# Passage from layer 2 to layer 3 of a four-layer graph network: attention vectors, half of the first attention sums, and the loads and casts of two weights moved to earlier places

## The reference, cut to what matters

```python
def _L2_gnn_ref(x, adj_matrix, bond_matrix, Wq, bq, Wk, bk, Wv, bv, Wo, bo, seq_len):
    q, k, v = (proj(Wq, bq), proj(Wk, bk), proj(Wv, bv))      # 8 heads of 64
    scores = jnp.einsum('bhqd,bhkd->bhqk', q, k) * SCALE
    mask = (adj_matrix + bond_matrix)[:, None, :, :]
    attn = jax.nn.softmax(scores * mask, axis=-1)
    ctx = jnp.einsum('bhqk,bhkd->bhqd', attn, v)
    return jnp.einsum('bse,fe->bsf', ctx.transpose(0, 2, 1, 3).reshape(...), Wo) + bo

def _L3_gnn_ref(X, A, Wv, bv, aw, ab, Wk, bk):
    Xw = X @ Wv + bv
    sj, si = Xw @ aw[:d, 0], Xw @ aw[d:, 0]
    e = jax.nn.leaky_relu(sj[:, None, :] + si[:, :, None] + ab[0], negative_slope=0.2)
    alpha_matrix = A * jnp.exp(e)
    transition = alpha_matrix / (jnp.sum(alpha_matrix, axis=-1, keepdims=True) + 1e-12)
    H, Xk = 0, X
    for k in range(3):
        H = H + Xk @ Wk[k] + bk[k]
        Xk = jnp.einsum('bij,bjd->bid', transition, Xk)
    return jax.nn.relu(H)
```

## Time and profile before

| what | value |
|---|---|
| runs, median of 3 | 2360.78 us |
| lowest and highest run | 2358.31 and 2362.7 us |
| the profiled execution | 2360.88 us |
| its span in the trace | 2359.1 us |
| mean granted TensorE clock | 0.996 |
| TensorE busy | 2323.2 us (98%) |
| VectorE busy | 1352.4 us (57%) |
| ScalarE busy | 798.0 us (34%) |
| POOL busy | 807.1 us (34%) |
| DMA, mean over the span | 89 GB/s |

### The profile page before, as it was taken

The page is one execution under the profiler, slowest core; times in us unless marked ns, Lnnn a source line. Parts: engine busy times, 40 slices in busy tenths (PEclk is TensorE's granted clock), DMA queues, the critical chain, the costliest instruction groups (busy, mean ns, idle before and its releaser), DMA issues. The chain is left out here.

```text
span 2359.1 us, 39284 instructions
## 1 busy us (share of the span) xinstructions
PE 2323.2 (98%) x15823; PEld 1898.6 (80%) x15823; DVE 1352.4 (57%) x2602; ACT 798.0 (34%) x1429; POOL 807.1 (34%) x995
## 2 busy tenths in 40 slices
PE   8999999999999999999999999999989999999998
PEld 5688888888888878888888888888768888888887
DVE  3565566566655654444555444555677667676753
ACT  3333333334333343333333333333332222223221
POOL 2454454445544524222333222333352222212120
PEclk9999999999999999999999999999999999999999
DMA  6323333333333333222223222222444333434330
GB/s 194 78 65 92 94 112 90 91 89 81 84 93 100 106 112 113 76 59 59 61 72 90 72 60 59 60 74 84 131 106 113 82 107 86 103 85 106 82 90 36
DMA packets 173477, 208.97 MB, mean 89 GB/s; under 512 B 64800, under 2 KB 81264, under 8 KB 173296
## 3 DMA queue, kind: packets, MB, share of 16 engines
q1 hardware_dynamic: 173296, 206.48, 31.7%
HBM read 88.91 MB, written 50.37 MB: 59 GB/s over the span
## 5 line engine op out<-in xcount | busy, mean ns | idle before, releaser
L328 PE MATMUL bank<-w_hi,h3T_hi 128*128 128x512 f32 x768 | 302.4, 394 | 0.0
L328 PE MATMUL bank<-w_lo,h3T_hi 128*128 128x512 f32 x768 | 299.5, 390 | 0.0
L328 PE MATMUL bank<-w_hi,h3T_lo 128*128 128x512 f32 x768 | 299.4, 390 | 0.0
L613 DVE TENSOR_TENSOR Z_lo<-bank,Z_hi 128x512 fp32r<-128x512 f32 x128 | 87.2, 682 | 192.4 <-ACT Z_hi L956 192.4
L328 PEld LDWEIGHTS bank<-w_lo,h3T_hi 128*128 128x128 f32 x768 | 144.4, 188 | 30.3
L328 PEld LDWEIGHTS bank<-w_hi,h3T_hi 128*128 128x128 f32 x768 | 144.5, 188 | 30.2
L328 PEld LDWEIGHTS bank<-w_hi,h3T_lo 128*128 128x128 f32 x768 | 144.4, 188 | 30.2
L956 ACT ACTIVATE Z_hi<-bank 128x512 fp32r<-128x512 f32 x128 | 76.0, 596 | 252.9 <-PE bank L328 163.3
L613 DVE TENSOR_TENSOR cT_lo<-bank,cT_hi 128x256 fp32r<-128x256 f32 x128 | 44.7, 408 | 203.7 <-ACT cT_hi L956 203.7
L646 DVE STREAM_TRANSPOSE hs<-hn 128x512 f32<-128x512 f32 x192 | 123.5, 687 | 58.1 <-ACT hn L970 58.1
L1203 POOL TENSOR_TENSOR h3T_lo<-hGA,h3T_hi 128x512 fp32r<-128x512 f32 x64 | 82.6, 1326 | 206.1 <-ACT h3T_hi L956 206.1
(11 more groups left out here) (231 smaller groups left out, 6053.5 us busy)
## 6 DMA issues: line engine op xcount, KB each, us to landing
hGA<-hs SPq DMA_DIRECT2D x768, 64.0 KB, 2.0
mid<-x SPq DMA_DIRECT2D x32, 1024.0 KB, 4.8
x<-mid SPq DMA_DIRECT2D x32, 1024.0 KB, 5.8
x<-in_x SPq DMA_DIRECT2D x16, 1024.0 KB, 5.9
hGB<-hs SPq DMA_DIRECT2D x256, 64.0 KB, 2.0
out<-x SPq DMA_DIRECT2D x16, 1024.0 KB, 5.4
blk<-in_adj SPq DMA_DIRECT2D x128, 64.0 KB, 2.9
adj<-in_adj SPq DMA_DIRECT2D x64, 64.0 KB, 4.1
```

The lines of the kernel that those rows point to most:

```text
L328: ins = eng.matmul(b[:], h[l][:, k, ts], W[r][:, k, :], start=(k == 0 and i == 0), stop=(last and k == 3 and i == 2))
L613: return eng.tensor_tensor(lo, src, hi.bitcast(F), ALU.subtract)
```

## The change

Nothing is computed otherwise; operations change their places in the programs of VectorE, ScalarE, POOL and SP. TensorE's program is as before.

- VectorE, iteration 15: the attention vectors and `cst` stand first, ahead of `l2_ctx(14, 0)` and the statistics. `l3_sums(0, (0, 1))` stands behind `l2_ctx(14, 1)`, ahead of output (14,1) and the softmax, and writes its unused product to sc3; `l3_sums(0, (2, 3))` stands ahead of V's evictions. Before, all of them stood between V's evictions.
- VectorE, iteration 16: `adj_T(3, 0)` and `l3_alpha(0)` stand behind the transposes of (3,1), ahead of outputs (15,2) and (15,3). Of group 1's sums two tiles stand behind the outputs, the third behind the row sum of group 0, the fourth behind T_lo of group 0.
- VectorE, layer 3, group 0: `adj_T(3, 1)` and `l3_alpha(1)` stand ahead of the transposes of (3,2) and the last `l3_zlo`.
- ScalarE: the hi parts of W3[2] and W3[1] are cast between the two halves of the last softmax's exponents; before, W3[2] behind the ptc copies, W3[1] behind the second norm. `l3_exp(0)` stands right behind that norm. The hi features of (3,0) wait for the first four sums.
- POOL: the lo part of W3[1] is made ahead of `l3_alpha(0)`.
- SP: W3[2] and W3[1] are asked ahead of the gather of (3,0). `rows3` is cut in two: `sums_out3(0)` and the adjacency blocks stand in iteration 15 behind the store of x, ahead of the load of W3[0]; `sums_in3(0)` stands in iteration 16.

```diff
             for g in range(NG + 1):
                 on, prev = g < NG, g >= 1
-                if prev:
-                    l2_ctx(g - 1, 0)
-                else:
-                    l01_recip(NG - 1)
-                    l01_x2(NG - 1, range(4))
-                stats_A(*(after2(g) if on else (3, 1)))
                 if g == NG - 1:
                     dve.wait_ge(d_vec3, 64)
...
                     eng.tensor_tensor(cst, cst, abc, ALU.add).then_inc(v_cst, 1)
                 if prev:
+                    l2_ctx(g - 1, 0)
+                else:
+                    l01_recip(NG - 1)
+                    l01_x2(NG - 1, range(4))
+                stats_A(*(after2(g) if on else (3, 1)))
+                if prev:
                     l2_out(g - 1, 0)
                 if on:
                     transposes(*after2(g))
                 if prev:
                     l2_ctx(g - 1, 1)
+                if g == NG - 1:
+                    l3_sums(dve, eng, 0, (0, 1))
...
                     elif u == 0:
                         transposes(3, 1)
+                        adj_T(3, 0)
+                        l3_alpha(0)
                 if not on:
-                    adj_T(3, 0)
-                    l3_alpha(0)
-                    l3_sums(dve, eng, 1, range(4))
+                    l3_sums(dve, eng, 1, (0, 1))
                 if on:
                     dve.wait_ge(d_bv2, 16)
+                    if g == NG - 1:
+                        l3_sums(dve, eng, 0, (2, 3))
...
-                        if g == NG - 1 and t >= 1:
-                            l3_sums(dve, eng, 0, ((0,), (1,), (2, 3))[t - 1])
...
                     if g == 0 and t == 0:
                         l3_rowsum(0)
+                        l3_sums(dve, eng, 1, (2,))
                     if g == 0 and t == 1:
                         l3_tlo(0)
+                        l3_sums(dve, eng, 1, (3,))
...
                     if t == 3 and g + 2 < NG:
+                        if g == 0:
+                            adj_T(3, 1)
+                            l3_alpha(1)
                         transposes(3, g + 2)
                     l3_zlo(1, ("z1", g, t), g, t)
-                if g + 1 < NG:
+                if g and g + 1 < NG:
                     adj_T(3, g + 1)
-                l3_alpha(g + 1)
+                    l3_alpha(g + 1)
...
+            first = g == 0 and 0 in ts
             if g == 0:
-                dve.wait_ge(*bank.done(("qk", NG - 1, 3)))
+                dve.wait_ge(v_cst, 1)
+                if not first:
+                    dve.wait_ge(*bank.done(("qk", NG - 1, 3)))
...
-                    dve.wait_ge(v_dotA, 8 * g + 2 * t + c - 1)
-                    eng.scalar_tensor_tensor(yt[c][:] if g < 2 else junk[:, c, :], hn[t][:], 0.0, arow[:, c, :], ALU.max, ALU.mult,
+                    dve.wait_ge(v_dotA, 8 * g + 2 * t + c - (not first))
+                    unused = sc3[:] if first else yt[c][:] if g < 2 else junk[:, c, :]
+                    eng.scalar_tensor_tensor(unused, hn[t][:], 0.0, arow[:, c, :], ALU.max, ALU.mult,
...
                 if not on:
                     norm_A(3, 1)
+                    l3_exp(0)
...
                 if on:
                     l2_exp(g, 0)
-                if on:
+                    if g == NG - 1:
+                        split_in_place(W3[2], d_w2)
+                        split_in_place(W3[1], d_w1)
                     l2_exp(g, 1)
-                else:
-                    split_in_place(W3[1], d_w1)
-                    l3_exp(0)
...
-                    act.wait_ge(v_cst, 1)
+                    act.wait_ge(v_dotA, 4)
                     features2_hi(3, 0, hT3[0])
...
-                if g == NG - 1:
-                    split_in_place(W3[2], d_w2)
...
+            split_in_place(W3[1], "w1")
             l3_alpha(0)
-            split_in_place(W3[1], "w1")
             l3_rowsum(0)
...
-            def rows3(g):
+            def sums_out3(g):
                 if g < NG:
                     sp.wait_ge(v_sc, g + 1)
                     eng.dma_start(si_dr[g].rearrange("(t p) -> p t", p=128), scol[g % 2][:, :, 1], allow_slow_non_contiguous=True).then_inc(d_sc, 16)
+
+            def sums_in3(g):
+                if g < NG:
                     sp.wait_ge(d_sc, 16 * (g + 1))
...
+                if g == NG - 1:
+                    sp.wait_ge(*bank.done(("k2", g, 3)))
+                    eng.dma_start(W3[2]["raw"][:], rows(L3_gnn_Wk[2])).then_inc(d_w2, 16)
+                    eng.dma_start(W3[1]["raw"][:], rows(L3_gnn_Wk[1])).then_inc(d_w1, 16)
                 if g == 0:
                     sp.wait_ge(v_x2, 4 * NG)
                     store_x(kA(0, NG - 1), mid[0][NG - 1])
                 if on:
                     gather(*after2(g))
-                if g == NG - 1:
-                    sp.wait_ge(*bank.done(("k2", g, 3)))
-                    eng.dma_start(W3[2]["raw"][:], rows(L3_gnn_Wk[2])).then_inc(d_w2, 16)
-                    eng.dma_start(W3[1]["raw"][:], rows(L3_gnn_Wk[1])).then_inc(d_w1, 16)
                 if g == NG:
-                    load_blocks(3, 0)
-                    rows3(0)
+                    sums_in3(0)
                     gather(3, 1)
                 if prev:
                     sp.wait_ge(v_x3, 4 * g)
                     store_x(kA(2, g - 1), mid[1][g - 1])
                 if g == NG - 1:
+                    sums_out3(0)
+                    load_blocks(3, 0)
                     sp.wait_ge(*bank.done(("pT", g, 3)))
                     eng.dma_start(W3[0]["raw"][:], rows(L3_gnn_Wk[0])).then_inc(d_w0, 16)
...
-                rows3(g + 1)
+                sums_out3(g + 1)
+                sums_in3(g + 1)
```

## The result

| | before | after |
|---|---|---|
| median of 14 runs | 2360.81 us | 2357.26 us |
| lowest and highest | 2358.31, 2362.7 us | 2351.14, 2359.18 us |
| the profiled execution | 2360.88 us | 2352.77 us |

The ratio is 0.9980, with a 95% interval of 0.9973 to 0.9986: 3.5 us faster, where 11.8 had been forecast. The spread tells more than the median. The 14 runs after fall into two groups with nothing between them: four at 2351.1 to 2352.8 us, ten at 2356.5 to 2359.2. The profile shows an execution of the shorter group, so it alone does not explain the median.

What follows compares the result with a forecast made beforehand. TensorE, busy 2323 of 2359.1 us, bounds the kernel, so only its idle and slow time can be won: 6.1 + 0.7 + 5.0 + 0.4 = 12.2 us off 2360.88 gives 2348.7, stated as 2349.0, range 2345.5 to 2355.0.

Steps and rivals of the forecast that it cites:

- Code still comes late: Rival: code for context (15,1) still late, o2(15,0) starts as before, later gains mostly hold; 2353.4 us, chance 0.12.
- Stall (a): TensorE's 4.41 us stop inside context (15,1), laid to cT_lo or late code; output o2(15,0) starts sooner, gaining 6.1 us.
- It moves the waits only: Rival: each wait feeds the next, so less than 4.7 us are won; 2358 us, chance 0.05.
- si's round trip: Store and read-back of si ahead of group 1's row sum in layer 3; rows landed by 1751.5 to 1753 us.
- row sum 1: Row sum of layer 3's group 1, waiting for alpha(1); the wait stays near 2.3 us, 0.4 us won.
- Attention vectors, W1, W2 and the gather: Vectors moved into VectorE's idle time, W2 and W1 asked 20 us sooner, gather of (3,0) sooner; vectors cost nothing.
- First sums: Sums (0,1) ahead of VectorE's last softmax, (2,3) ahead of V's evictions; cost taken as 0, at most 3.3 us.
- Row sum 0: Row sum of layer 3's group 0, waiting for alpha(0); wait falls from 1.43 to about 0.7 us, gaining 0.7 us.
- The hop: TensorE's first hop in layer 3, waiting for T_lo; its wait and half clock behind it go, gaining 5.0 us.
- the first rival: Row sum of layer 3's group 1 waits over 3 us and the clock falls; 2351.3 us, chance 0.2.
- Collision of sums and POOL: Rival: VectorE's sums slow beside POOL, 1.08 us more each, T_lo late, hop waits 4.6 us; 2355.5 us, chance 0.06.
- arow late: Rival: VectorE blocks on arow at the head of its softmax, delaying context (15,0); 2365.6 us or more, chance 0.02.

Runs made afterwards that it cites:

- e1: The changed kernel once more with no edit: 2358.32 us, 11 runs, three at 2350.2 to 2352.3 and eight at 2358.3 to 2360.4.
- e2: The changed kernel with the load of W3[0] asked about 8 us later, ahead of the gather of (3,1): 2358.25 us, nine of 11 runs long.
- e6: The changed kernel with group 0's adjacency block loads issued only behind context (15,1), the si store left early: 2361.42 us, 11 of 12 runs long.
- e10: The changed kernel with W2 and W1 asked and cast where they were before, plus 32 identity transposes at TensorE's start: 2348.42 us, ratio 0.9944.
- e3: The changed kernel with W2 and W1 asked and cast where they were before: 2352.6 us in 10 runs, ratio 0.9967.
- e11: The kernel before the change with 32 identity transposes added at TensorE's start: 2361.11 us, 11 runs, ratio 0.9999.
- e9: The changed kernel with 32 identity transposes at TensorE's start and POOL's two bias sums moved behind the scales of (3,2): 2348.84 us.
- e12: The changed kernel with 32 identity transposes at TensorE's start and the second half of the first sums behind V's evictions: 2352.57 us.
- e5: The changed kernel with group 0's si store issued only behind context (15,1), which also let the adjacency loads go out sooner: 2352.3 us, five runs.
- e7: The changed kernel with both group 0's si store and its adjacency block loads issued only behind context (15,1): 2354.86 us, six runs.
- e16: The changed kernel with 8 identity transposes (16 instructions) added at TensorE's start: 2351.4 us, five runs from 2350.5 to 2351.6.
- e17: The changed kernel with two 1 MB memory-to-memory copies added ahead of the si store: 2353.4 us, five runs from 2352.4 to 2354.1.
- e4: The kernel before the change with its first four transposes done nine times, shifting later code by 64 instructions: 2366.18 us.

## Why the prediction was wrong, point by point

**Verdict.** The forecast of 2349.0 us in a range from 2345.5 to 2355.0 missed the median of 2357.26. The direction was right, and the four short executions (2351.1 to 2352.8) lie in the range; the long ones make the median. The step that failed is in the rivals: "Code still comes late, as x(14)'s store and W0 still fill the queues", with a chance of 0.12 and a time of 2353.4. Stall (a)'s gain of 6.1 us takes it for granted that the code is in time. It was late in 18 of 25 executions, by another cause than the one named, and it cost more. The sign that the prediction gave for it, a stall inside the context at instruction packets, is what e1 shows. The rival "It moves the waits only" (2358, chance 0.05) comes near the median by its number alone: where the code is in time, 8.1 us were won.

**Why the cause was missed.** I took the full queues (1.05, 386 GB/s) for what delayed the code, and counted megabytes: "2 MB of 4 are gone". e2 took another megabyte away from the place and changed nothing. What decides in the change is the si store, 2 KB in 512 scattered pieces. I had followed it as a term of si's round trip only, and so put its effect on the code at nothing. The change brought it to 0.5 us behind pT(15,0), close to where the next block of TensorE's program moves, and in the long executions TensorE stood for 10.4 to 12.1 us. In the kernel before it was not the store: the late packet started at 1709.57 us, ahead of the store's issue at 1710.82. There the full queues remain the candidate, and no run tests them. Every DMA that a change moves sooner stands ahead of something else, and the queue of instructions is one of the things that it can stand ahead of.

**Its size.** 2353.4 was put together from the old stall of 4.4 us, though "comes late" has no reason to stay at 4.4. Measured in e1: 10.40 us (where the short execution waits 1.33 for cT_lo), then the half clock (0.58 from 1719.7 to 1726), less 1.7 us that row sum 1 waits less. The long group lies 6 to 8 us above the short one.

**The rule that was weighed.** The Trainium skill ("Runtime: NRT & Kernel Launch", Instruction fetch mechanics) calls a border's cost mostly hidden. In e1 and e6 a border cost 10.40 and 12.13 us, so the measurement decides against it for this place. That I let the rule pull the chance of this rival down was a mistake, as the row spoke the other way.

**Attention vectors, W1, W2 and the gather: nothing.** Right in size: the vectors hid in VectorE's idle time, though the loads landed 0.4 us later against pT than in the profile before. e10 shows that W1 and W2 are worth nothing. That they were harmless was wrong: with them early (the change and e1) 18 of 25 executions are long, with them late (e3) none of 10.

**First sums: nothing.** Nearly right. One of the second four took 1.52 us, and V's last eviction ended 2.83 us behind pT(15,0), where I had 1.85. So the contexts waited for V and started 3.09 us behind pT(15,0) in place of 2.85: 0.24 us.

**Stall (a), 6.1 us.** Right where the code is in time: o2(15,0) starts 6.52 us behind pT(15,0), where I had 6.25. That the old stall had two candidate causes which end together was in the text, and e11 bears it out: the block in time alone gives nothing.

**Row sum 0, 0.7 us.** Under by 0.7: the wait is gone altogether. The norm did stand behind POOL's scales, for 2.22 us, but these were done 12.9 us behind pT(15,0) where it had been 14.6 before, and POOL's product of alpha ended at 1725.11 us, 0.05 ahead of the row sum. It is gone by that little.

**The hop, 5.0 us.** Right: no wait and no half clock behind it.

**Row sum 1, 0.4 us won.** Predicted 52.05 us behind pT(15,0), measured 52.86, a wait of 3.13 us in place of 2.3. That is the first rival (0.2), down to the half clock behind it. That si's round trip is the limit was half right: in the change POOL's chain of bias sums, features and scales ended a little later, and without it si's was next (e9).

**Collision of sums and POOL, arow late:** arow was not late. Of group 1's sums the fourth tile's two took 1.68 and 1.77 us beside POOL's split of W0, behind T_lo, where nothing waited for them, so the collision cost nothing. The Trainium skill's rule on two SBUF inputs ("SBUF — State Buffer", Who interferes with whom) agrees with these, with the 1.52 us beside POOL's product, and with e12, where four sums beside POOL's features took 1.56 to 1.75 us each and TensorE waited 5.0 us for cT_lo behind them.

**What stays open.** Why the block is in time in 7 of 25 executions of the change, and why e3 is never hit, is not settled. In the short execution the packet started 2.6 us before the si store was issued; in e1 nothing moved in that stretch, on any queue, and the packet did not start. So it must have been held or asked late before the store was there, and no run shows by what; the store can account only for what follows. The moment does vary where the block is in time: the packet starts 2.1 us ahead of pT(15,0) in e5, 0.3 ahead in e7, 1.5 behind in e3. A race between such a request and the store, whose first pieces move 1.4 us behind pT(15,0) in both executions, would fit this and e16, and is argued. Traffic ahead of the store softens the stall (e17). No trace shows when the block is asked, only when its packet moves.

## What to carry to other kernels

Where TensorE stands still inside a run of small matmuls and no semaphore explains it, look for the instruction packets and for the small scattered DMAs beside them, and shift the code by a few instructions at a place where the engine waits anyway: it is the cheapest test there is, and here it was the cure too. When one stall has two candidate causes, price the change for each of them alone. When the times of a kernel fall into two groups, a profile of one execution explains only the group that it comes from.

## What the runs showed of the hardware that was not expected

- A store of 2 KB as 512 scattered values, issued near the moment at which TensorE's next block of code is due, went with stalls of 10.40 us (e1) and 12.13 us (e6), while the data queue took 20.5% of the engines' time (e2). With the store behind the contexts no stall was seen (e5, e7); without the adjacency loads behind the store the stall stayed (e6).
- The same store slows an ordinary load too. The 1 MB of W3[0] landed 5.4 us after their issue with the store behind them (e5), and 13.3 us after it with the store 1.4 us ahead of them and no other load between (e6).
- Two steps of 64 small matmuls use up 256 instructions in 2.1 us, where 128 matmuls of 512 columns with their weight loads last some 29 us (0.226 us from start to start). The stalls for code all stand among the small ones: at the same matmul (13041) in the kernel before and in e1, e2, e6 and e17, and at 12791, in a score step, in e4.
- 16 instructions more at the start of the program, which do nothing for the result, went with a median 7 us lower (e16, five runs, against e1).
